# A gated cross-attention decoder on one core: the engines' group loops written out in a row

## The reference

```python
x = x + tanh(g_xattn[0]) * xattn0(layernorm(x), ctx, W, b)        # one head: (xW'+b)(cW'+b)', softmax, times ctx
x = x + tanh(g_ffn[0])   * ffn0(layernorm(x), w_up, w_down)       # ternary weights, rms norm, erf gelu, 512 -> 2048 -> 512
x = x + tanh(g_xattn[1]) * xattn1(layernorm(x), ctx, mask, ...)   # 16 heads of 32, with biases
x = x + tanh(g_ffn[1])   * ffn1(layernorm(x), gate_w, up_w, down_w, s_in, s_in_down)   # silu(gate) * up, then down
```

## Time and profile before

| | |
|---|---|
| median of 3 runs | 1810.36 us (1810.17 to 1814.83) |
| the profiled execution's own time | 1809.43 us |
| its span, first to last instruction | 1807.6 us |
| mean granted TensorE clock | 0.905 |
| PE busy | 1353.0 us, 8120 matmuls |
| DVE busy | 1422.8 us, 2437 instructions |
| ACT busy | 692.1 us, 2105 instructions |
| POOL busy | 240.5 us, 197 instructions |

### The profile page before, as it was taken

How to read it: one execution, slowest core, us unless ns; L and a number is a source line. 1 busy time by engine, 2 the same in 40 slices (tenths; PEclk the granted TensorE clock), 3 DMA queues, 4 the chain that set the end, 5 groups by cost and what they waited for, 6 DMA issues and landing times.

```text
span 1807.6 us, 24307 instructions
## 1 busy us (share of the span) xinstructions
PE 1353.0 (75%) x8120; PEld 699.1 (39%) x8120; DVE 1422.8 (79%) x2437; ACT 692.1 (38%) x2105; POOL 240.5 (13%) x197
## 2 busy tenths in 40 slices
PE   5044747799787978698778978797879886988663
PEld 3021315344453436343533345343634453434321
DVE  6988896878787687778687878768778878786695
ACT  2113206451464227432645146422734164425210
POOL 1002200131003200230013100320013001310000
PEclk9556868899899989999889999999989999999888
DMA  9165761042102320141004210232023200420011
GB/s 350 66 238 156 193 143 36 7 88 63 44 1 61 68 59 14 35 87 53 26 7 88 60 48 1 61 68 59 14 35 73 68 25 7 88 59 24 7 29 47
DMA packets 267433, 120.08 MB, mean 66 GB/s; under 512 B 244090, under 2 KB 244602, under 8 KB 265750
## 3 DMA queue, kind: packets, MB, share of 16 engines
q1 hardware_dynamic: 267286, 118.27, 25.7%
HBM read 49.04 MB, written 8.39 MB: 32 GB/s over the span
## 4 chain that ended last, share of the span: by engine, by line
issue 43%; DVE 26%; PE 21%; DMA 3%; ACT 3%; SPq 2%; POOL 2%; POOLq 0%; DVEq 0%; ACTq 0%
PE bank L1074 15%; PE bank L1163 5%; DVE amax L825 2%; DVE pair L834 2%; DVE th L867 2%; DVE hid L830 2%; SPq L303 1%; ACT region L534 1%; DMA hqt<-pair 1%; DVE pair L842 1%; DVE pair L849 1%; DVE hid L871 1%; DVE pair L844 1%; DVE sc L796 1%; DVE stats L685 1%
## 5 line engine op out<-in xcount | busy, mean ns | idle before, releaser
L1163 PE MATMUL bank<-w_dn,region 128*128 128x512 fp8e4 x1024 | 243.1, 386 | 36.8 <-DMA region<-region 36.8
L1074 PE MATMUL bank<-w_up,xt 128*128 128x512 fp8e4 x1024 | 245.6, 388 | 32.8 <-ACT region L498 17.5
L1074 PE MATMUL bank<-w_gate,xqt 128*128 128x512 bf16 x512 | 147.2, 415 | 127.9 <-DVE th L867 84.1
L507 ACT ACTIVATE th<-bank,half_cg 128x512 f32<-128x512 f32 x128 | 88.0, 687 | 347.4 <-PE bank L1074 347.4
L425 POOL TENSOR_TENSOR region<-g,region 128x512 f16<-128x512 f32 x128 | 177.8, 1394 | 298.9 <-ACT region L498 291.1
L867 DVE SCALAR_TENSOR_TENSOR th<-th,bank 128x512 f32<-128x512 f32 x128 | 87.6, 685 | 133.5 <-ACT th L507 133.5
L534 ACT ACTIVATE region<-bank,nm 128x77 f32<-128x77 f32 x512 | 160.2, 346 | 67.6 <-DVE nm L913 67.6
L1074 PE MATMUL bank<-w_down,hqt 128*128 128x512 bf16 x512 | 132.4, 418 | 56.2 <-DMA hqt<-pair 56.2
L495 ACT ACTIVATE g<-bank 128x512 f32<-128x512 f32 x128 | 76.4, 597 | 245.4 <-PE bank L1074 186.3
L1163 PEld LDWEIGHTS bank<-w_dn,region 128*128 128x128 f16 x1024 | 101.1, 99 | 162.4 <-issue 45.1
L1074 PEld LDWEIGHTS bank<-w_up,xt 128*128 128x128 f16 x1024 | 101.2, 100 | 161.5 <-issue 51.8
(11 more groups left out here) (206 smaller groups left out, 2469.8 us busy)
## 6 DMA issues: line engine op xcount, KB each, us to landing
xin<-in_x SPq DMA_DIRECT2D x16, 512.0 KB, 4.0
out_x<-x SPq DMA_DIRECT2D x16, 512.0 KB, 3.0
region<-in_w_up_t SPq DMA_DIRECT2D x1, 4096.0 KB, 12.8
hid<-in_gate_w SPq DMA_DIRECT2D x4, 1024.0 KB, 5.3
x<-in_gate_w SPq DMA_DIRECT2D x4, 1024.0 KB, 6.3
hid<-in_up_w SPq DMA_DIRECT2D x4, 1024.0 KB, 5.2
x<-in_up_w SPq DMA_DIRECT2D x4, 1024.0 KB, 5.6
hid<-in_down_w SPq DMA_DIRECT2D x4, 1024.0 KB, 4.8
```

Of the source, the lines that this page charges most:

```text
L507: eng.activation(th[:, u % 2, :], bank[4][:, :], ACT.Tanh, scale=half_cg[:, :]).then_inc(sg["th"], 1)
L1074: last = mm(out, lhs, rhs, start=(n == 0), stop=(n == len(pairs) - 1))
L1163: last = mm(bank[2 + t % 2][:, :], ht[i][:, t % 2, f, :], w_dn[:, f, :], start=(f == 0 and i == 0), stop=(f == KF - 1 and i == 1))
```

## The change

The five loops on the engines become Python loops, so that the six bodies stand one behind the other with g as a number, and every wait is for a constant. With the loops go the count of DVE's steps per iteration (`DVE_STEPS`; `steps` is one running count) and the increments of the three `passed` semaphores. No work instruction, buffer, order or wait on another engine's progress is changed.

```diff
--- before.py
+++ after.py
@@ -76,7 +76,6 @@
 HT_AFTER = {3: 0, 4: 1, 6: 2, 8: 3}
 WT_AT = [16 * (TILES * min(m, 2 * PIECES) + max(m - 2 * PIECES, 0)) for m in range(len(FP4_PIECES) + 1)]
 WT_DONE = WT_AT[-1]
-DVE_STEPS = 141
 RADD = bass.bass_isa.ReduceOp.add
 RMAX = bass.bass_isa.ReduceOp.max
 
@@ -204,7 +203,7 @@
 
         names = ("pool_step pool_const dve_step loaded_small loaded_w0 loaded_w0t loaded_b0 loaded_kv loaded_q "
                  "loaded_o loaded_up loaded_dn loaded_piece0 loaded_piece1 split wout_hi wout_lo ctx_psum ctx_done tern_part tern_done wsum_all "
-                 "wmax_part wmax_all pe_passed dve_passed piece_read piece_codes wt_done sp_passed tanh_done").split()
+                 "wmax_part wmax_all piece_read piece_codes wt_done tanh_done").split()
         per = dict(xin=32, var1=1, var2=1, var3=1, var4=2, rstd1=1, rstd2=1, rstd3=1, rstd4=2,
                    xn1=4, xn2=4, xn3=4, tr1=4, tr2=4, tr3=4, xh1=4, xh2=4, xh3=4, xl1=4, xl2=4, xl3=4,
                    sc1=4, nm1=4, ex1=4, p1t=4, p1h=4, p1l=4, o1=4, x1=4,
@@ -307,10 +306,8 @@
                 done = ("ht_even", "ht_odd")[t % 2]
                 for i, made in enumerate(("hh", "hl")):
                     want(sp, made, g, CHUNKS * (t + 1))
-                    sp.sem_inc(sm["sp_passed"])
                     if t >= 2 and i == 0:
                         want(sp, "dn", g, t - 1)
-                        sp.sem_inc(sm["sp_passed"])
                     sp.dma_start_transpose(ht[i][:, t % 2], hn[i][:, t % 2]).then_inc(sg[done], 16)
 
             for m, (n, i) in enumerate(FP4_PIECES):
@@ -366,7 +361,7 @@
                 turn_h(g, 3)
                 store(g, 1)
 
-            with sp.Fori(0, GROUPS - 2) as g:
+            for g in range(GROUPS - 2):
                 turns(g, g + 1, g + 2)
             turns(GROUPS - 2, GROUPS - 1, None)
             turns(GROUPS - 1, None, None)
@@ -438,7 +433,7 @@
             pool.wait_ge(sm["wmax_all"], 3)
             eng.partition_all_reduce(red[:, 2:5], wmax[:, :], P, RMAX).then_inc(sm["wsum_all"], 1)
             phase_b(0, None, 1)
-            with pool.Fori(0, GROUPS - 2) as g:
+            for g in range(GROUPS - 2):
                 phase_a(g, g + 1)
                 phase_b(g + 1, g, g + 2)
             g = GROUPS - 1
@@ -563,7 +558,7 @@
 
             phase_a(None, 0)
             phase_b(0, None)
-            with act.Fori(0, GROUPS - 2) as g:
+            for g in range(GROUPS - 2):
                 phase_a(g, g + 1)
                 phase_b(g + 1, g)
             g = GROUPS - 1
@@ -579,15 +574,15 @@
         @block.vector
         def _(dve):
             eng = nc.vector
-            steps = [0, 0]
+            steps = [0]
 
             def done(ins):
 
-                steps[1] += 1
+                steps[0] += 1
                 ins.then_inc(sm["dve_step"], 1)
 
             def settle():
-                dve.wait_ge(sm["dve_step"], steps[0] + steps[1])
+                dve.wait_ge(sm["dve_step"], steps[0])
 
             def split(hi, lo, src):
                 done(eng.tensor_copy(hi, src))
@@ -688,7 +683,6 @@
                 s = 1 if stage == 4 else 0
                 ts = slice(tiles[0], tiles[-1] + 1)
                 settle()
-                dve.sem_inc(sm["dve_passed"])
                 for t in tiles:
                     done(eng.bn_aggr(mv[:, s, t, :], stats[:, s, t, :]))
                 settle()
@@ -1034,13 +1028,9 @@
             phase_b(0, None, 1)
             dve.wait_ge(sm["piece_read"], len(FP4_PIECES))
             dve.wait_ge(sm["wt_done"], WT_DONE)
-            pro = steps[1]
-            with dve.Fori(0, GROUPS - 2) as g:
-                steps[0], steps[1] = g * DVE_STEPS + pro, 0
+            for g in range(GROUPS - 2):
                 phase_a(g, g + 1)
                 phase_b(g + 1, g, g + 2)
-                assert steps[1] == DVE_STEPS, steps[1]
-            steps[0], steps[1] = (GROUPS - 2) * DVE_STEPS + pro, 0
             g = GROUPS - 1
             phase_a(g - 1, g)
             phase_b(g, g - 1, None)
@@ -1144,7 +1134,6 @@
                     want(pe, "xl2", g)
                 else:
                     want(pe, "hh", g, s - 1)
-                pe.sem_inc(sm["pe_passed"])
                 ts = slice(t * P, (t + 1) * P)
                 product(bank[s % 2][:, :], [(xt[i][:, k, ts], w_up[:, k, n * D:(n + 1) * D]) for k in range(KD)
                                             for i in range(2)]).then_inc(sg["up"], 1)
@@ -1280,7 +1268,7 @@
             phase_b(0, None)
             pe.wait_ge(sm["piece_codes"], len(FP4_PIECES))
             pe.wait_ge(sm["wt_done"], WT_DONE)
-            with pe.Fori(0, GROUPS - 2) as g:
+            for g in range(GROUPS - 2):
                 phase_a(g, g + 1)
                 phase_b(g + 1, g)
             g = GROUPS - 1
```

## The result

The changed kernel takes 1787.2 us in the median of 4 runs (1784.7 to 1791.7), the kernel before 1812.6 beside it (1810.2 to 1823.5): a ratio of 0.9857, 95% interval 0.9833 to 0.9882. The forecast was 1790, 1785 to 1797. Its profiled execution took 1785.0 us, with a span of 1782.9, which is 24.7 us under the span of before. Run again later it took 1787.7 us, ratio 0.9868 (0.9847 to 0.9889). The gain forecast was 20.3 us; against the kernel before beside it, it was 25.4 us the first time and 21.6 the second.

The account below looks back on a forecast made before the run. No engine was full; DVE's jump back at each loop seam was taken to lie on the path. Terms summed to 20.9 us, a lap check gave 19.7; the middle, 20.3, gave 1789.1, forecast as 1790 us, range 1785 to 1797.

Parts of the forecast that it names:

- (1): DVE's jump back, between out4 and the first score maximum: its wait goes, 2.32 us a lap, 11.6 us.
- (2): Rest of phase A up to sdev: shorter as PE idles less and keeps its clock, 0.62 us a lap, 3.1 us.
- (3): A group's last transposing DMA up to down4: no longer slowed by ACT's code fetch, 0.5 us a lap, 2.5 us.
- (4): The down4 product behind that DMA: 0.4 us a lap less, called the clock's luck, 2.0 us.
- (5): Waits for constants, increments and register sums gone: 1.2 us for register waits, 0.5 us (0 to 3) for increments.
- (6): Clock in the middle of a lap, sdev to the second L406: cost 0, bounds 1.5 us a group either way.
- (7): Code: the program grows by five bodies, but fetching it was taken to cost 0.
- Rival C: Slower: written-out code arrives late at block boundaries, costing 39 us less the 20.3, 1829 us; chance 0.02.
- B: Rival at the seam: something behind DVE's jump gives no time back, only 1.7 us goes, 1809 us; chance 0.03.
- Rival A: Clock takes part back by long middles and slow down4 in every group: 9.3 us left, 1801 us; chance 0.12.
- Rival D: Favourable side: short middles, best down4 and the whole of (3) in every group, 5.7 us more, 1784 us; chance 0.05.

Follow-up runs that it names:

- the fill at the seam: Kernel before, loops kept, plus 14 matmuls that nobody reads in PE's idle at the seam of two iterations: 1819.4 us in a single execution.
- the two fills: Changed kernel plus unread matmuls ahead of each group's last down4 and in the tail: 1784.8 us; with the other long PE idle stretches filled too: 1789.1 us.

## Why the prediction held, step by step

- The signs named beforehand came: laps of 191 to 193 us, no "issue" wait at L907 or on ACT, L907 0.67 us behind L878, PE idle 1.12 us with the granted clock at 1.00 behind it, 4.43 to 4.45 us from L339 to `down4` at four of five seams, 96.01 us in phase B.
- Steps (1) and (2), 14.7 us forecast, 14.3 measured in five laps. (1) is shown three ways: DVE's loop alone, the hints, and three of five jumps removed. (2) is shown by the fill at the seam.
- Steps (3) and (4), 4.5 us forecast, 4.1 measured. (3) alone measured 1.9 us for 2.5: it is the packet of code in the transfer, put there by ACT's jump at four seams and by code run straight on at the first. The prediction's reading, the same DMA engines, is what the packets show. (4) stayed what it was called, the clock's, 2.2 us for 2.0.
- Step (5) is the term of the sum that was mis-sized. I took 1.2 us for register waits and 0.5, at most 3, for the increments, by looking for them on the chain of the transposing DMAs. The ones that count stand on PE, in front of the `up` and `down` products: by the medians all together are worth 6 us, those of PE alone 4 to 5, which is outside the bound of 3. Only 1 us of it is seen on the path; the rest, as far as the profiles show, is where the clock falls, and no term of the sum had that. For the register waits, the hinted loops with increments took 1795.5 us and written-out code with increments 1793.1 and 1793.7, ratios 0.9903 against 0.9905 and 0.9908: no difference that these runs can tell. The trace has 26.05 us for a middle in a loop and 25.96 written out with increments, 0.09 us a group, and with the 0.2 of phase B 1.2 us fits.
- Step (6) at nothing: two long middles fewer (one of seven, for three) gave the profiled execution 3 us. Whether this was luck is open: the second profile of the change has one long middle of seven too, and its time of 1789.4 comes from longer rests of phase B. "Nothing in the change governs it" was said without a run that shows it.
- Step (7) at nothing: DVE, ACT and PE show no wait of size with "issue" in the written-out code, and PEld the same ones as before. Rival C is out, and so is B.
- Rival A (1801) did not come; the same kernel scatters from 1784 to 1792 us. Rival D (1784) is what its best runs show.
- The forecast of 20.3 us against 24.7 between the profiles: the 4.4 us are (6), 3.0 us, and what is left, 3.4 for the 1.7 of (5), less 0.9 that (1) to (4) fell short, and 0.6 by which the forecast was set below its own sum. The jumps, steps (1) to (4), carry 18.4 of the 24.7 us. By the ratios, the fetch at the jumps and what hangs on it is 17 to 18 us (hints, 1 - 0.9903; 14 to 21 by the interval), and the increments are 6 by the medians and 7 by the ratios of the two runs side by side.

## What to carry to other kernels

In this kernel DVE and ACT waited at every jump back for the first instructions of their loop, and the kernel paid most for the engine whose next instruction was on the path: DVE, 2.3 us plus the clock that PE lost in that time. ACT's wait was covered, but its packet of code made a transfer on the path 0.6 us longer. If code size matters, hint the jump; that gave most of the gain with the loops left in. Where one copy of the body is already written out behind a loop, the profile of before holds both prices, and laps cut at one mark read them off; and an instruction without effect between a wait and its matmul is not free on the path.

## What the runs showed of the hardware that was not expected

- An increment between a wait and the matmul behind it costs 0.09 us on PE's path (1.98 us of idle for 1.89).
- A packet of code of 8 KB that starts 3.63 to 3.70 us behind the issue of a transposing DMA makes it land 0.6 us later (4.9 us for 4.3); at 3.72 to 3.74 us it costs 0.2 us at most.
- A hint at the start of a loop's body took DVE's wait at the jump back from 2.3 us to none.
- Filling idle time of the changed kernel gained nothing: the fall came in another idle stretch, or in what the fill had left of one, and of the two fills the one with the higher mean clock was not faster (0.931 and 1789.1 us, 0.905 and 1784.8).
- Parts of a lap in which the clock doesn't fall repeat almost to the hundredth between two profiles of the change (37.04 to 37.07 us, 25.82 us). Parts in which it falls differ by up to 2.5 us (rests of phase B 117.2 to 119.7), also where their mean clock is the same 0.96.
